# One transfer for the last context rows of four batches, and q moved by batch over 128 partitions

## The chip, the cores and the metric

The kernel runs on one core of a Trainium2 chip. The metric is the device time of that core in microseconds. Of the kernel before there are three runs: 1287.83, 1288.2 and 1289.85 us, with a median of 1288.2 us.

## What is computed

The input `x` has 128 batches of 32 rows by 1024 columns, all in float32. Three layers follow one another, each with a residual, and each reads the layer norm of the running sum:

```python
x = x + xattn(layernorm(x), ctx_1024, ctx_1024, 0, mask)
x = x + s4(layernorm(x), Lambda, p, q, Vc, Ct, Bp, D, log_step)
x = x + ffn(layernorm(x), A_w, B_w, Wq_w, keys)

# xattn: 32 heads of 32 columns, 8 groups of keys and values, 257 context rows of 256 columns a batch
scores = einsum('bsgrd,btgd->bgrst', xq, xk) / sqrt(32) + mask
out = einsum('bgrst,btgd->bsgrd', softmax(scores), xv)
# s4: a causal convolution over the last axis with one kernel of 1024 numbers, made from the parameters
# ffn: 64 experts of rank 8, gated by a top-16 router, between two dense products
```

The change touches the first layer alone: the last (257th) context row of each batch, and the way the normalised rows `xq` come into the layout that the scores need.

## The kernel before

A tile is 128 rows: four batches of 32. There are 32 tiles. The program is written out by hand for each engine, in an `iteration(it, odd)` that each engine runs for `it` from 2 to 30, with hand-ordered calls before and behind it. An iteration works on several tiles at once: scores and exponentials of tile `it`, the output and the convolution of tile `it - 1`, the experts of tile `it - 2`, and loads and layer norm of tiles `it + 1` and `it + 2`. Engines wait for each other only by semaphores, each in the order in which its calls stand.

- **SyncE issues every transfer**, one after the other, each once its semaphores allow. In an iteration this is the order around the change: `load_last(it + 1)` (L404), `store_q(it + 1)` (L391), `load_keys(it + 1, 0)` (L365), `move_q(it + 1)` (L397), `load_keys(it + 1, 1)`, `load_context(it, 3)` (L358), `load_keys(it + 1, 2)`, `load_x(it + 2)` (L384), `load_context(it, 1)`.
- **The last context row** of a batch is not in the score matmuls, which take 256 rows. `load_last` brings it into `vl`, repeated over the batch's 32 partitions. GpSimd multiplies it with `xq` in `last_product` (L1087, the product itself is L1093) and uses it again in `last_share` (L1136). `vl` has two halves, used in turn, and `load_last(tile)` waits for the last use of the half two tiles before, among others `tm_done` of `residual`, on GpSimd.
- **q**: ScalarE normalises `xq` in place (`q_norm`, L854). `store_q` writes it to the DRAM tensor `turn_q` (batch, row, column). `move_q` waits for that and reads it back into `qx`, where partition 32 c + s holds quarter c of row s, for the four batches one after the other: 4 KB a partition in pieces of 1 KB. VectorE's `q_turn(tile, h)` (L1391, the transpose is L1394) waits for all of `q_moved`, ScalarE's `q_high` and GpSimd's `q_low` (L1084) split the result in two parts `qs`, and TensorE's `scores(it, b)` (L574) multiplies them with the keys `kt`.
- **VectorE's other work** near `q_turn`: `maximum(it, n)` (L1387), which takes a 256-wide maximum of the scores for ScalarE's `exp` (L840), and `q_stats(tile, k)` (L1417), which waits for the load of `xq` of a later tile. In an iteration `q_turn(it + 1, 0)` stands between `maximum(it, 24)` and `maximum(it, 25)`, and `q_stats(it + 2, 0)` between `maximum(it, 27)` and `maximum(it, 28)`.

A transfer raises its semaphore by 16 when it is through, so the waits count 64 for four transfers.

Of the kernel before, what the change touches and what calls it, by code (L numbers as in the profile page):

```python
# [22 lines left out]
BATCHES, SEQ, DIM = 128, 32, 1024  # L23
CTX_LEN, CTX_DIM = 257, 256
# [3 lines left out]
P = 128  # L28
BPT = P // SEQ
TILES = BATCHES // BPT  # L30
HALVES = 2
GPH = GROUPS // HALVES
# [68 lines left out]
def at(tile, per, k):  # L101

    return tile * per + k
# [8 lines left out]
def build(nc, io):  # L112
    ctx = ExitStack()
    with ctx:
        def sb(name, shape, dt=F32):
            return ctx.enter_context(nc.sbuf_tensor(name, shape, dt))

        def sem(name):
            return ctx.enter_context(nc.semaphore(name))
# [12 lines left out]
        qx = sb("qx", [P, BPT, HALVES, REP, HEAD_DIM])  # L132
# [19 lines left out]
        vl = sb("vl", [P, 2, CTX_DIM])  # L152
# [27 lines left out]
        turn_q = nc.dram_tensor("turn_q", [BPT, SEQ, DIM], F32, kind="Internal").ap()  # L180
# [7 lines left out]
        q_moved = sem("q_moved")  # L188
# [6 lines left out]
        vl_loaded = sem("vl_loaded")  # L195
# [74 lines left out]
        context = io["ctx_1024"]  # L270
# [44 lines left out]
        def _(sp):  # L315
# [81 lines left out]
            def move_q(tile):  # L397
                sp.wait_ge(q_stored, at(tile, 16, 16))
                if at(tile, 2, 0) > 0:
                    sp.wait_ge(qr_done, at(tile, 2, 0))  # L400
                for quad in range(GPH):
                    sp.dma_start(qx[SEQ * quad:SEQ * (quad + 1), :, :, :, :].rearrange("p b h r d -> p b (h r d)"),
                                 turn_q.rearrange("b s (q c) -> s b q c", q=GPH)[:, :, quad, :]).then_inc(q_moved, 16)

            def load_last(tile):
                if at(tile, 4, -5) > 0:
                    sp.wait_ge(tm_done, at(tile, 4, -5))
                if at(tile, 2, -1) > 0:
                    sp.wait_ge(lp_done, at(tile, 2, -1))
                for c in range(BPT):  # L410
                    sp.dma_start(vl[SEQ * c:SEQ * (c + 1), tile % 2, :],
                                 context[tile * BPT + c:tile * BPT + c + 1, 2 * P, :]
                                 .broadcast_to([SEQ, CTX_DIM])).then_inc(vl_loaded, 16)

            def store_last(tile):
                sp.wait_ge(lm_done, at(tile, 2, 2))
# [25 lines left out]
            def iteration(it, odd):  # L442
                turn_last(it)
                if on(it - 3):
                    store(it - 3)
                if on(it - 1):
                    move_den(it - 1, 2)
                    load_context(it - 1, 2)
                    load_residual(it - 1)
                load_context(it, 0)  # L450
                if on(it - 1):
                    move_den(it - 1, 3)
                if on(it + 1):
                    load_last(it + 1)
                    store_q(it + 1)
                    load_keys(it + 1, 0)
                    move_q(it + 1)
                    load_keys(it + 1, 1)
                load_context(it, 3)
                if on(it + 1):  # L460
                    load_keys(it + 1, 2)
                if on(it + 2):
                    load_x(it + 2)
                load_context(it, 1)
                move_den(it, 1)
                if on(it + 1):
                    store_last(it + 1)
                move_den(it, 0)
                if on(it + 1):
                    load_keys(it + 1, 3)  # L470
            load_x(0); load_router(); load_mask(); load_s4(); load_wide(); load_weight(0); load_weight(1)
            load_last(0); load_context(0, 2); clear_kernel(); load_keys(0, 0); load_context(0, 0); load_weight(2)
            store_q(0); load_keys(0, 1); load_last(1); move_q(0); load_x(1); load_weight(3); load_keys(0, 2)
            store_last(0); load_keys(0, 3); turn_last(0); store_q(1); load_weight(4); load_keys(1, 0); load_weight(5)
            move_q(1); load_keys(1, 1); store_last(1); move_den(0, 0); load_keys(1, 2); load_context(0, 3)
            load_context(0, 1); load_x(2); load_context(1, 0); move_den(0, 1); load_weight(6); load_keys(1, 3)
            load_weight(7); turn_last(1); move_den(0, 2); load_keys(2, 0); load_residual(0); move_den(0, 3)
# [567 lines left out]
        def _(pool):  # L1045
# [40 lines left out]

            def last_product(tile, h):  # L1087
                if h == 0:
                    pool.wait_ge(vl_loaded, at(tile, 64, 64))
                pool.wait_ge(xq_used, at(tile, 2, 2))  # L1090
                pool.wait_ge(lm_done, at(tile, 2, h))
                v = vl[:, tile % 2, :].rearrange("p (q h d) -> p h q d", q=GPH, h=HALVES)[:, h, :, :].unsqueeze(1).broadcast_to([P, REP, GPH, HEAD_DIM])
                pool.tensor_tensor(lastp[:, :, :, :], xq[:].rearrange("p (q h r d) -> p h r q d", q=GPH, h=HALVES, r=REP)[:, h, :, :, :], v, ALU.mult).then_inc(lp_done, 1)  # L1093
# [53 lines left out]
            def iteration(it, odd):  # L1147
# [19 lines left out]
                if on(it + 1):  # L1167
                    last_product(it + 1, 0)
                    last_sum(it + 1, 0)
                    last_mask(it + 1, 0)  # L1170
# [3 lines left out]
                if on(it + 1):  # L1174
                    last_product(it + 1, 1)
                k_low(it, 3)
                if on(it + 1):
                    last_sum(it + 1, 1)
                    last_mask(it + 1, 1)
                    q_low(it + 1, 0)  # L1180
                    k_low(it + 1, 0)
            row_scale(0, 0); last_product(0, 0); last_sum(0, 0); last_mask(0, 0); last_product(0, 1); last_sum(0, 1)
            last_mask(0, 1); k_low(0, 0); k_low(0, 1); q_low(0, 0); row_scale(0, 1); q_low(0, 1); k_low(0, 2)
            last_product(1, 0); last_sum(1, 0); last_mask(1, 0); last_shift(0, 0); last_product(1, 1); last_sum(1, 1)
# [511 lines left out]
```

## Time and profile before

| | us |
|---|---|
| median of three runs | 1288.2 |
| runs | 1287.83 to 1289.85 |
| the profiled execution's own time | 1290.52 |
| its span | 1288.6 |
| TensorE busy | 1232.9 (96%) |
| VectorE busy | 959.7 (74%) |
| ScalarE busy | 1122.9 (87%) |
| GpSimd busy | 825.4 (64%) |
| transfers, mean share of 16 DMA engines (main queue) | 40.9% |

The span runs from the first to the last instruction of the program; the profiled execution took 1.9 us more than its span and 2.3 us more than the median of the runs. Busy time is what an engine spent in instructions; register, semaphore and DMA-issuing instructions don't count. A share is an average over stages with different limits, so the stages have to be read one by one.

### The profile page before, as it was taken

What the parts mean: (1) busy time and instruction counts of PE and PEld (TensorE: products, weight loads), DVE (VectorE), ACT (ScalarE), POOL (GpSimd) and SP (SyncE); (2) the same over time, 40 slices, a digit from 0 to 9 for tenths busy, and PEclk for the clock granted to TensorE, in tenths of its full rate; (3) what the DMA queues carried; (4) which work ended last, traced back from release to release, by engine and by line L of the source; (5) the groups of instructions that cost most, each with busy time, mean ns of one, the idle gap of its engine ahead of it and who ended that gap; (6) DMA issues with size and microseconds to landing.
All of it is one profiled execution on the core that took longest, in us unless ns stands there. A gap on an engine that the chain in (4) does not pass through costs nothing.

```text
span 1288.6 us, 41515 instructions
## 1 busy us (share of the span) xinstructions
PE 1232.9 (96%) x13676; PEld 1083.1 (84%) x13676; DVE 959.7 (74%) x3424; ACT 1122.9 (87%) x3337; POOL 825.4 (64%) x1259
## 2 busy tenths in 40 slices
PE   3679999999999999999999999999999999999997
PEld 2558888888888888888888888888888888888886
DVE  6977777777777777877777777677777877877753
ACT  5889999998999999999999999989999999999841
POOL 4447676776667677666767766676777666777520
PEclk9979999999999999999999999999999999999999
DMA  7443443443344444434544433453443344444210
GB/s 237 134 127 93 151 155 122 130 133 125 119 148 152 124 130 132 129 123 141 155 122 131 147 124 118 134 154 123 131 151 123 122 128 154 132 125 132 61 60 33
DMA packets 150103, 166.38 MB, mean 129 GB/s; under 512 B 58217, under 2 KB 116082, under 8 KB 149890
## 3 DMA queue, kind: packets, MB, share of 16 engines
q1 hardware_dynamic: 149890, 163.72, 40.9%
q8 instruction: 112, 1.84, 0.6%
q14 instruction: 101, 0.83, 0.2%
HBM read 128.50 MB, written 34.08 MB: 126 GB/s over the span
## 4 chain that ended last, share of the span: by engine, by line
PE 76%; DVE 5%; DMA 4%; POOL 4%; ACT 4%; issue 3%; SPq 2%; DVEq 0%; ACTq 0%; POOLq 0%
PE ps_p L562 22%; PE ps_p L633 15%; PE ps_p L661 12%; PE ps_p L648 12%; PE ps_p L594 8%; PE ps_s L574 7%; ACT pr L840 2%; DMA dn<-den 2%; DMA xq<-in_x 1%; POOL lastp L1093 1%; DVE ms L1387 1%; SPq L381 1%; ACT pts L772 1%; DMA vl<-in_ctx 1%; POOL lastp L1103 1%
## 5 line engine op out<-in xcount | busy, mean ns | idle before, releaser
L840 ACT ACTIVATE pr<-ms,negmax 128x256 f32<-128x256 f32 x1024 | 512.6, 504 | 17.3 <-DVE negmax L1387 17.3
L1387 DVE CUSTOM_DVE_ANT_0 ms<-ps_s,neg_mask,last 128x256 f32<-128x256 f32 x1024 | 447.0, 473 | 7.1 <-PE ps_s L574 6.2
L772 ACT ACTIVATE pts<-ps_p 128x512 f32<-128x512 f32 x512 | 298.3, 590 | 45.8 <-PE ps_p L562 29.1
L562 PE MATMUL ps_p<-ident,pr 128*128 128x128 f32 x2048 | 296.5, 280 | 10.4 <-ACT pr L840 5.1
L562 PEld LDWEIGHTS ps_p<-ident,pr 128*128 128x128 f32 x2048 | 229.1, 142 | 48.0 <-issue 17.4
L840 ACT ACTIVATION_READ_ACCUMULATOR pr<-ms,negmax 128x1 f32 x1024 | 199.6, 195 | 0.0
L1061 POOL TENSOR_TENSOR kt<-kr,kt 128x512 fp32r<-128x512 f32 x128 | 164.9, 1288 | 24.1 <-ACT kt L772 24.1
L648 PE MATMUL ps_p<-wa_hi,ut_hi 128*128 128x288 f32 x512 | 159.6, 312 | 1.4 <-DVE ut_lo L1203 1.4
L648 PE MATMUL ps_p<-wa_lo,ut_hi 128*128 128x288 f32 x512 | 151.8, 296 | 0.0
L648 PE MATMUL ps_p<-wa_hi,ut_lo 128*128 128x288 f32 x512 | 151.7, 296 | 0.0
L1203 DVE TENSOR_TENSOR ut_lo<-ps_p,ut_hi 128x512 fp32r<-128x512 f32 x128 | 87.7, 690 | 74.8 <-ACT ut_hi L772 74.5
L1103 POOL TENSOR_TENSOR lastp<-lastp 128x256 f32<-128x256 f32 (+4 forms) x320 | 128.1, 400 | 22.7
L594 PE MATMUL ps_p<-pts,cx 128*32 128x128 f32 x4096 | 139.8, 277 | 2.8 <-DVE wb_lo L1215 2.3
L633 PE MATMUL ps_p<-strip_hi,ut_hi 128*128 128x512 f32 (+2 forms) x384 | 135.5, 353 | 0.0
L574 PE MATMUL ps_s<-kt,qs 32*128 32x256 f32 x3072 | 128.1, 297 | 5.3 <-DVE negmax L1387 3.0
L633 PE MATMUL ps_p<-strip_hi,ut_lo 128*128 128x512 f32 (+2 forms) x384 | 133.1, 347 | 0.0
L633 PE MATMUL ps_p<-strip_lo,ut_hi 128*128 128x512 f32 (+2 forms) x384 | 132.9, 346 | 0.0
L1084 POOL TENSOR_TENSOR qs<-qr,qs 128x512 fp32r<-128x512 f32 x64 | 82.6, 1290 | 69.6 <-ACT qs L772 69.6
L574 PEld LDWEIGHTS ps_s<-kt,qs 32*128 32x128 f32 x3072 | 101.9, 187 | 28.6 <-issue 24.9
L594 PEld LDWEIGHTS ps_p<-pts,cx 128*32 128x32 f32 x4096 | 105.0, 110 | 24.8 <-issue 21.5
L1136 POOL TENSOR_TENSOR tmp<-vl,dn 128x512 f32<-128x512 f32 x64 | 69.1, 1079 | 80.6 <-DVE dn L1447 80.6
L772 ACT ACTIVATE ut_hi<-ps_p 128x512 fp32r<-128x512 f32 x128 | 75.3, 592 | 51.0 <-PE ps_p L562 50.9
(139 smaller groups left out, 2584.6 us busy)
## 6 DMA issues: line engine op xcount, KB each, us to landing
cx<-in_ctx SPq DMA_DIRECT2D x128, 256.0 KB, 3.9
kr<-in_keys SPq DMA_DIRECT2D x128, 256.0 KB, 3.0
xq<-in_x SPq DMA_DIRECT2D x32, 512.0 KB, 4.3
turn_q<-xq SPq DMA_DIRECT2D x32, 512.0 KB, 2.9
qx<-turn_q SPq DMA_DIRECT2D x128, 128.0 KB, 2.9
xr<-in_x SPq DMA_DIRECT2D x32, 512.0 KB, 3.9
out_x<-tmp SPq DMA_DIRECT2D x32, 512.0 KB, 3.2
dn<-den SPq DMA_DIRECT2D x512, 2.0 KB, 2.3
```

The source lines that it names most:

```text
L562: mm = pe.transpose(into[:, j * P:(j + 1) * P], source, ident[:, :])
L574: mm = pe.matmul(ps_s[:, quad, h * SW:(h + 1) * SW], qs[rs, it % 2, q_part, b, h, :, :].rearrange("p r s -> p (r s)"), kt[rs, b, k_part, h ...
L594: mm = pe.matmul(product("o", b, it)[HEAD_DIM * q:HEAD_DIM * (q + 1), h * P:(h + 1) * P], cx[:, b, j, g * HEAD_DIM:(g + 1) * HEAD_DIM], pt ...
L633: mm = pe.matmul(product("y", k, tile)[:, o0:512], u[:, c, :], s[:, s0:s0 + w], start=(c == 0 and j == 0), stop=(c == 4 * k + 3 and j == 2 ...
L648: mm = pe.matmul(product("f", k, tile)[:, 0:ZB], u[:, c, :], w[:, c, k * ZB:(k + 1) * ZB], start=(c == 0 and j == 0), stop=(c == FC - 1 an ...
L661: mm = pe.matmul(product("b", k, tile)[:, :], u[:, c, :], w[:, c, k * 512:(k + 1) * 512], start=(c == 0 and j == 0), stop=(c == BC - 1 and ...
L772: return act.activation(out, in_, ACT.Copy, scale=scale)
L840: act.activation(pr[:, b % 2, g, :], ms[:, n % MS, :], ACT.Exp, bias=negmax[:, n % MS:n % MS + 1], scale=-1.0, accum_out=den[:, b, g:g + 1 ...
L1061: pool.tensor_tensor(kt[:, b, 1, :, :], kr[:, at(tile, BPT, b) % KRS, :, :], kt[:, b, 0, :, :].bitcast(F32), ALU.subtract).then_inc(kl_don ...
L1103: pool.tensor_tensor(near, near, far, ALU.add).then_inc(ls_done, 1)
L1203: return dve.tensor_tensor(lo, source, hi.bitcast(F32), ALU.subtract).then_inc(done, 1)
L1387: dve.tensor_tensor_reduce(ms[:, n % MS, :], ps_s[:, g % GPH, g // GPH * SW:(g // GPH + 1) * SW], neg_mask[:, 0:SW], 1.0, last[:, it % 2, ...
```

## The change

`move_q` has four transfers as before, but each now brings one batch to all 128 partitions, where each brought one quarter of the columns of all batches to 32 partitions. The pieces are the same 512 of 1 KB a tile. The source of a transfer is now written with the quarter `q` outermost (4 entries), then the row `s` (32), then 256 columns; it was the row outermost (32), then the batch (4), then 256 columns.

`load_last` now has one transfer a tile where it had four. The source is 4 batches outermost, each repeated 32 times with a step of zero, then 256 columns; the destination is 128 partitions. It was 32 repeats of one row to 32 partitions. GpSimd's wait counts 16 a tile now, not 64.

```diff
-                for quad in range(GPH):
-                    sp.dma_start(qx[SEQ * quad:SEQ * (quad + 1), :, :, :, :].rearrange("p b h r d -> p b (h r d)"),
-                                 turn_q.rearrange("b s (q c) -> s b q c", q=GPH)[:, :, quad, :]).then_inc(q_moved, 16)
+                for b in range(BPT):
+                    sp.dma_start(qx[:, b, :, :, :].rearrange("p h r d -> p (h r d)"),
+                                 turn_q[b, :, :].rearrange("s (q c) -> q s c", q=GPH)).then_inc(q_moved, 16)
...
-                for c in range(BPT):
-                    sp.dma_start(vl[SEQ * c:SEQ * (c + 1), tile % 2, :],
-                                 context[tile * BPT + c:tile * BPT + c + 1, 2 * P, :]
-                                 .broadcast_to([SEQ, CTX_DIM])).then_inc(vl_loaded, 16)
+                sp.dma_start(vl[:, tile % 2, :],
+                             context[tile * BPT:(tile + 1) * BPT, 2 * P, :].unsqueeze(1)
+                             .broadcast_to([BPT, SEQ, CTX_DIM])).then_inc(vl_loaded, 16)
...
-                    pool.wait_ge(vl_loaded, at(tile, 64, 64))
+                    pool.wait_ge(vl_loaded, at(tile, 16, 16))
```

On SyncE, in an iteration, these are the transfers around the two places before; the sizes are those of the destination, partitions first.

```order
L381 DMA dn<-den 32x16 x4
L411 DMA vl<-in_ctx 32x256 x4
L395 DMA turn_q<-xq 128x1024
L369 DMA kr<-in_keys 128x512
L402 DMA qx<-turn_q 32x4x256 x4
L369 DMA kr<-in_keys 128x512
L362 DMA cx<-in_ctx 128x2x256
L369 DMA kr<-in_keys 128x512
L389 DMA xq<-in_x 128x1024
```

And this is the same place with the change:

```order
L381 DMA dn<-den 32x16 x4
L410 DMA vl<-in_ctx 128x1x256
L395 DMA turn_q<-xq 128x1024
L369 DMA kr<-in_keys 128x512
L402 DMA qx<-turn_q 128x1x256 x4
L369 DMA kr<-in_keys 128x512
L362 DMA cx<-in_ctx 128x2x256
L369 DMA kr<-in_keys 128x512
L389 DMA xq<-in_x 128x1024
```

Nothing stands in another place: three issues a tile are gone, and the order of the rest is the same. The other engines' instructions are unchanged.

## Rows read from the trace of the kernel before

**Rows 1.** The page, section 1: busy us, share of the span, instructions.
```profile
PE 1232.9 (96%) x13676; PEld 1083.1 (84%) x13676; DVE 959.7 (74%) x3424; ACT 1122.9 (87%) x3337; POOL 825.4 (64%) x1259
```
**Rows 2.** Busy time by stretch; the header gives the columns.
```profile
core 0: us, PE busy (x) PEld busy (x) DVE busy (x) ACT busy (x) POOL busy (x), PEclk, DMA share, GB/s
...
103.00:1196.00 1093.00, 1089.30 (x12305) 961.95 (x12304) 833.33 (x3038) 1002.84 (x3015) 749.72 (x1139) 1.00 0.43 133
```
**Rows 3.** Waits in total; SyncE's own first: us, times, longest.
```profile
SPq L411 <- POOL tmp L1136: 189.0, 30, 7.3
...
POOL lastp L1093 <- DMA vl<-in_ctx: 9.4, 6, 7.6
...
PEld ps_s L574 <- POOL kt L1061: 3.7, 15, 0.6
```
**Rows 4.** Transfers issued: count, KB each, median us from issue to landing.
```profile
vl<-in_ctx SPq DMA_DIRECT2D x128, 32.0 KB, 1.8
```
**Rows 5.** Packets in 169.1:171.2, 651.05:652.85, 98.3:100.3; q1: packets, MB, share of 16 engines.
```profile
DMA packets 489, 0.45 MB, mean 216 GB/s; under 512 B 47, under 2 KB 489, under 8 KB 489
q1 hardware_dynamic: 489, 0.45, 72.3%
...
DMA packets 184, 0.14 MB, mean 79 GB/s; under 512 B 60, under 2 KB 183, under 8 KB 183
q1 hardware_dynamic: 183, 0.13, 23.0%
...
q1 hardware_dynamic: 100, 0.00, 2.7%
```
**Rows 6.** SyncE's timeline, tile 4 and tile 17: start us, us, transfer.
```profile
168.27 1.83 SPq L402 DMA_DIRECT2D qx<-turn_q  x4
...
656.22 1.76 SPq L402 DMA_DIRECT2D qx<-turn_q  x4
...
663.60 0.38 SPq L389 DMA_DIRECT2D xq<-in_x  x1
```
**Rows 7.** VectorE's timeline, the first use of q and of x: tiles 4, 17.
```profile
176.51 0.71 DVE L1394 STREAM_TRANSPOSE qr<-qx 128x512 f32<-128x512 f32 x1
...
179.52 0.69 DVE L1417 BATCH_NORM_STATS2 lns<-xq 128x6 f32<-128x512 f32 x1
...
664.87 0.71 DVE L1394 STREAM_TRANSPOSE qr<-qx 128x512 f32<-128x512 f32 x1
...
667.88 0.68 DVE L1417 BATCH_NORM_STATS2 lns<-xq 128x6 f32<-128x512 f32 x1
```
**Rows 8.** GpSimd's and TensorE's timelines behind them: end of q's split, next scores.
```profile
672.22 1.28 POOL L1084 TENSOR_TENSOR qs<-qr,qs 128x512 fp32r<-128x512 f32 x1 [0.57 <-ACT qs L772]
...
674.64 0.98 PE L574 MATMUL ps_s<-kt,qs 32*128 32x256 f32 x24
```
**Rows 9.** VectorE's and TensorE's timelines where x came late.
```profile
293.25 0.69 DVE L1417 BATCH_NORM_STATS2 lns<-xq 128x6 f32<-128x512 f32 x1 [1.45 <-DMA xq<-in_x]
...
298.08 0.63 PE L562 MATMUL ps_p<-ident,x 128*128 128x128 f32 x4 [0.32 <-DVE x L1462]
```
**Rows 10.** The first 20 us: busy time by stretch, then SyncE's timeline, then the chain.
```profile
10.00:18.00 8.00, 2.28 (x11) 2.31 (x12) 5.65 (x12) 5.29 (x8) 2.11 (x2) 1.00 1.04 371
18.00:20.00 2.00, 2.00 (x11) 1.88 (x11) 1.08 (x1) 0.60 (x1) 1.76 (x4) 1.00 0.59 204
...
5.78 3.15 SPq L411 DMA_DIRECT2D vl<-in_ctx  x4
...
11.72 8.77 DMA kr<-in_keys
```
**Rows 11.** Tile 1's q: SyncE's and VectorE's timelines, and busy time by stretch.
```profile
47.22 2.51 SPq L402 DMA_DIRECT2D qx<-turn_q  x4
...
54.55 0.71 DVE L1394 STREAM_TRANSPOSE qr<-qx 128x512 f32<-128x512 f32 x1
...
50.00:55.00 5.00, 3.35 (x54) 2.54 (x57) 4.86 (x22) 5.00 (x20) 1.64 (x3) 1.00 0.68 151
```

## The prediction

> **What bounds the kernel now.** I read the page first: TensorE is busy for 96% of the span, ScalarE for 87%, VectorE for 74% [rows 1]. Then the stretches: from 103 to 1196 us TensorE is busy for 1089.3 of 1093.0 us [rows 2]. So over 29 tiles of some 37.5 us only 3.7 us are lost; a time saved on another engine or queue is worth nothing there, and a delay costs only what is over its slack. Elsewhere (the first 100 us, before the pipeline is full) the transfers and VectorE count. Next SyncE's waits: it stood 189.0 us before `load_last`, waiting for GpSimd [rows 3]. A queue that waits so much is not short of issue time. Last the timelines around q, to see by how much each transfer is early.
>
> **What is removed: three issues a tile.** An issue takes some 0.43 us on SyncE (four in 1.76 us [rows 6]), so 3 x 0.43 = 1.3 us a tile. After `load_last` SyncE mostly waits for the next thing anyway, so I count zero. The one who may gain is GpSimd: it waited for `vl` 6 times, 9.4 us together, of which the start is 7.6 us [rows 3], and TensorE's weight loads waited for GpSimd's `kt` 3.7 us in 15 times. The rest, 1.8 us of GpSimd's waits, is the ceiling in the steady part; behind GpSimd there is slack again, so I take 0.3 us of TensorE's time.
>
> **What is changed: how the packets spread over the DMA engines.** The bytes and packets are the same. A q transfer now goes at a DMA share of 72.3%, counted over 16 engines, with other traffic small [rows 5], so its pieces lie on all of them. What the new patterns do is not in this trace: none of its transfers has a source with 4 entries outermost. The two bounds are 16 engines as now, and four engines, one for each outermost entry. Under the first nothing changes. I take the second, since the outermost entry is the natural unit to divide by (the old ones had 32 rows there), and since it is the bound that can hurt.
>
> The Trainium skill, "DMA: Bandwidth & Descriptors", section "Why a DMA increments its semaphore by 16 and not by 1", says that the number of engines is the largest number up to 16 that divides the slowest non-unit dimension of both patterns, which would be 4 here, the lowest four; its section "Rules for kernel authors" warns of just such a leading zero-stride broadcast. It speaks against this change; by it the four-engine bound holds, and no row of this trace shows it.
>
> **The price of a packet.** Small packets cost 2.7% x 16 x 2.0 us / 100 = 8.6 ns [rows 5]. A 1 KB packet of q costs (72.3% x 16 x 2.1 us - 47 x 0.0086) / 442 = 54 ns, one of `vl` (23.0% x 16 x 1.8 - 60 x 0.0086) / 123 = 50 ns. I take 52 ns. Bigger ones go by the full stretch: 371 GB/s over 16 engines [rows 10] is 23 GB/s each, 0.73 us for the 16 KB that an engine carries of a `kr` load, 1.47 us for its 32 KB of `xq`. What a transfer costs beside its packets is 1.8 us less two packets = 1.7 us, by `vl` [rows 4].
>
> **q, on four engines.** 512 packets on 4 engines are 128 each, 128 x 52 = 6.7 us, where it was 32 each. Last landing: 1.7 + 6.7 = 8.4 us behind the first issue. It is needed after 176.51 - 168.27 = 8.24 us in tile 4, after 664.87 - 656.22 = 8.65 us in tile 17 [rows 6, 7]. So VectorE waits for 0 to 0.2 us: the change eats the whole slack and stops there.
>
> **x, behind q on the same four engines.** `load_x` is issued 7.38 us after q [rows 6], and then these engines have still `kr`, `cx` (16 x 52 ns = 0.83 us) and `kr` to do: 8.4 + 0.73 + 0.83 + 0.73 + 1.47 = 12.1 us behind q's issue. It is needed after 11.25 us (tile 4) to 11.66 us (tile 17) [rows 6, 7]. VectorE, in order, then waits for 0.5 to 0.9 us, and its next maxima, ScalarE's exponentials and the second half of q come later by as much. What is late next is `scores(it + 1, 0)`: GpSimd has q's split ready at 672.22 + 1.28 = 673.50 us, TensorE begins at 674.64, a slack of 1.1 us [rows 8]. A case of it is in the trace: a wait of 1.45 us for x cost TensorE 0.3 us [rows 9], which is the same slack. So 0.5 to 0.9 us are covered, and the steady part costs **nothing**; if the cover were gone, each tile would pay all of it, some 20 us. With 50 ns the wait is 0.2 to 0.6 us, with 54 ns 0.8 to 1.2 us, the edge.
>
> **vl, on four engines.** 32 packets each, 1.7 us, against four issues over 1.3 us now: it lands at about the same time. Hidden, as now, by GpSimd's work of the tile before.
>
> **The start.** From 10 to 18 us all engines are full (share 1.04), then 0.59 [rows 10]. Four of them get 24 packets more from `vl` of tile 0: 24 x 52 ns = 1.25 us. The `kr` load that the chain runs through for 8.77 us [rows 10] is queued behind. Its bounds: 1.25 us later, or up to 2.0 us earlier, since SyncE's four issues took 3.15 us there and one takes at most 1.15. As the engines are full, an earlier issue only lengthens the queue: I take +1.25 us. Tile 1's q is issued at 47.22 and needed at 54.55, after 7.33 us [rows 11], so VectorE waits 1.1 us; but ScalarE is the full one there (5.00 of 5.00 us), fed by maxima already made. Bounds 0 to 1.1, I take 0, by that row.
>
> **Sum.** 1.25 - 0.3 + 0 = +1.0 us. The profiled execution took 1290.5 us and would take 1291.5; it stands 2.3 us over the median, so for the median 1288.2 + 1.0 = **1289.2 us**. Own range of this case 1287.0 to 1291.5 (below: no loss at the start and the 0.3 us; above: 1.25 and 1.1 us at the start, and an edge of 1 us over the slack in some tiles). What a measurement can tell from no change is 0.2%, 2.6 us.
>
> **The rivals.**
> - **The slack is overrun (slower).** Everything as above, but packets on four full engines cost more, or SyncE is held up behind their queues. It decides from a DMA wait of 1.1 us on VectorE a tile. For it: 54 ns already reaches 1.2 us. Against it: the engines then carry one stream, with little contention. At the wait of [rows 9] in each of 28 tiles: 28 x 0.3 = 9 us, 1288.2 + 1.25 + 9 = 1298.5 us. At 58 ns x would land at 8.4 + 0.8 + 3.8 = 13.0 us, a wait of 1.7, a loss of 0.6 us: 17 us, 1306 us. Chance 0.33.
> - **The pieces go to 16 engines as before (the change does only what saves issues).** For it: no row speaks against it. Then there is -0.3 us and nothing at the start: 1287.9 us. Chance 0.12.
> - **The start was short of issue time (faster).** The queue has a gap that the 2.0 us of SyncE's time fills, and `kr` lands up to 2.0 us earlier; with GpSimd's 1.8 us passed on in full: 1288.2 - 3.8 = 1284.4 us. The share of 1.04 speaks against it. Chance 0.08.
>
> **How the numbers follow.** The forecast has 0.47, of which 0.04 lies over +2.6 us. Slower is 0.33 + 0.04 = 0.37, faster 0.08, the same 0.43 + 0.12 = 0.55. The range leaves out the faster rival and the far end of the slower one, some 0.2 together: 1286.5 to 1300.
>
> **What would show it.** Right: q lands 8 to 8.8 us behind its first issue, the DMA share stays at a quarter in that stretch and not 72%; VectorE's wait for x goes from 10.5 us in all to 15 to 25 us, some small waits for q appear; TensorE stays busy for over 1088 us of 1093 in the same stretch; the first scores come 1 us later. Wrong: q's landing unchanged (16 engines); x's wait over 1.1 us in most tiles and TensorE waiting behind `qs`, `z` or the maxima; or an issue on SyncE that takes microseconds, because a queue is full.

## The result and the profile after

The changed kernel takes **1301.7 us** in the median of four runs (1296.34 to 1301.99), the kernel before 1288.0 (1285.33 to 1289.85): a ratio of **1.0098, 95% interval 1.0066 to 1.013**. Timed again later it was 1.0120 (1.0094 to 1.0145). So it is slower by some 14 to 16 us, and the forecast of 1289.2 us is wrong; 1301.7 lies outside its range of 1286.5 to 1300.0. The profiled execution took 1301.71 us, with a span of 1299.9, against 1290.52 and 1288.6 before: 11.3 us longer.

The page of the changed kernel, section 1, answers to [rows 1]; under it the busy time of the stretch of [rows 2]:

```profile
PE 1237.5 (95%) x13676; PEld 1083.0 (83%) x13676; DVE 959.0 (74%) x3424; ACT 1126.0 (87%) x3337; POOL 825.7 (64%) x1259
```
```profile
103.00:1196.00 1093.00, 1081.88 (x12208) 951.36 (x12207) 826.11 (x3006) 994.40 (x2977) 742.31 (x1124) 1.00 0.42 131
```

TensorE is idle for 11.1 us of the stretch, where it was for 3.7, and gets through 97 matmuls fewer (12208 against 12305, 0.8%). The loss is in the steady part. TensorE's timelines of before (the first two rows) and of the changed kernel (the last two) show where the scores of tile 3 and of tile 31 begin:

```profile
148.93 0.98 PE L574 MATMUL ps_s<-kt,qs 32*128 32x256 f32 x24
...
1199.11 0.98 PE L574 MATMUL ps_s<-kt,qs 32*128 32x256 f32 x24
```
```profile
147.77 0.98 PE L573 MATMUL ps_s<-kt,qs 32*128 32x256 f32 x24
...
1210.68 0.98 PE L573 MATMUL ps_s<-kt,qs 32*128 32x256 f32 x24
```

These 28 tiles took 1050.18 us and take 1062.91: +12.7 us, or 0.45 us a tile. What lies before them and behind them did not lose: 1288.6 - 1050.2 = 238.4 us before, 1299.9 - 1062.9 = 237.0 now.

Over just these 28 tiles, the same work in both, TensorE's idle time goes from 3.7 us (1050.18 less 1046.49 busy) to 11.1 (1062.91 less 1051.80), 7.4 us more. The rest is busy time, and it lies in the matmuls of one line, L633 before and L632 now, which multiply `strip` with the two halves of `ut` for the convolution. Their rows, first before, then after (us; busy us of matmuls and of weight loads; granted clock, DMA share, GB/s):

```profile
148.93:1199.11 1050.18, 191.94 (x1008) 166.24 (x1008) 1.00 0.43 133
```
```profile
147.77:1210.68 1062.91, 197.77 (x1008) 167.46 (x1008) 1.00 0.42 131
```

They are busy for 5.8 us more. Together that is 13.2 us, all of the 12.7. The tile read below shows why both belong to one place.

The chain of waits, by engine, first before and then after:

```profile
PE 76%; DVE 5%; DMA 4%; POOL 4%; ACT 4%; issue 3%; SPq 2%; DVEq 0%; ACTq 0%; POOLq 0%
```
```profile
PE 54%; DMA 16%; ACT 9%; DVE 6%; issue 5%; POOL 5%; SPq 5%; DVEq 0%; ACTq 0%; POOLq 0%
PE ps_p L561 16%; PE ps_p L632 11%; PE ps_p L647 9%; DMA qx<-turn_q 7%; PE ps_p L593 7%; PE ps_p L660 6%; ACT pr L839 5%; PE ps_s L573 5%; DMA turn_q<-xq 3%; DMA xq<-in_x 3%; DMA dn<-den 2%; SPq L402 2%; SPq L381 2%; ACT xq L853 2%; ACT pts L771 1%
```

TensorE held three quarters of the chain and holds half. The transfers of q (`qx<-turn_q`) have 7% of it; before they were not among its lines. The waits in total (engine, line, what it waited for: us, times, longest) answer to [rows 3]; lines behind `load_last` are one lower than before:

```profile
DVE qr L1393 <- DMA qx<-turn_q: 20.9, 24, 2.5
DVE lns L1416 <- DMA xq<-in_x: 10.1, 14, 4.6
PE ps_p L632 <- DVE ut_lo L1202: 9.5, 15, 1.5
POOL lastp L1092 <- DMA vl<-in_ctx: 8.6, 1, 8.6
```

The first line is new. VectorE waits for q in most tiles, 20.9 us in all. The third is new too: TensorE waits for `ut_lo`, a product of VectorE that has nothing to do with q. VectorE's wait for x is no longer than before over the whole run (10.5 us there); in the stretch of [rows 2] it is 5.6 us in 13 times, against 4.7 in 8. What the forecast took for the next thing late, TensorE's scores waiting for q's split, is in no row. GpSimd waits for `vl` only once, at the start.

**One tile read through.** Tile 8's q in the changed kernel, from the timelines of SyncE, VectorE and TensorE (start us, us, engine, line, operation; in brackets the idle time before it and what ended it):

```profile
320.24 2.26 SPq L402 DMA_DIRECT2D qx<-turn_q  x4
...
328.82 0.28 PE L632 MATMUL ps_p<-strip_hi,ut_lo 128*128 128x256 f32 x1
...
328.84 0.71 DVE L1393 STREAM_TRANSPOSE qr<-qx 128x512 f32<-128x512 f32 x1 [1.84 <-DMA qx<-turn_q]
...
329.85 0.69 DVE L1202 TENSOR_TENSOR ut_lo<-ps_p,ut_hi 128x512 fp32r<-128x512 f32 x1
...
330.59 0.49 PE L632 MATMUL ps_p<-strip_hi,ut_hi 128*128 128x512 f32 x1 [1.49 <-DVE ut_lo L1202]
```

q lands 328.84 - 320.24 = 8.6 us behind its first issue. VectorE has been standing in front of its transpose for 1.84 us. Behind the transpose in its queue come `maximum(it, 25)` and then `u_low(it - 1, 1)`, which makes the second half of `ut_lo` for the convolution of the tile before. That ends at 330.54, and TensorE, through with the first half at 329.10, starts the second at 330.59. Before, in tile 17, the same pieces stood like this:

```profile
665.88 0.68 DVE L1203 TENSOR_TENSOR ut_lo<-ps_p,ut_hi 128x512 fp32r<-128x512 f32 x1
...
666.85 0.28 PE L633 MATMUL ps_p<-strip_hi,ut_lo 128*128 128x256 f32 x1
666.97 0.39 PE L633 MATMUL ps_p<-strip_hi,ut_hi 128*128 128x512 f32 x1
```

`ut_lo` was ready at 666.56 and was used at 666.97: **0.4 us of slack** (0.34 to 0.42 us in tiles 3 to 29 of this trace). I had not looked at this place.

The last matmul of the first half and the first of the second half stand 0.12 us apart here (666.85 and 666.97) and 1.77 us apart in the tile above (328.82 and 330.59). So the wait costs 1.65 us where the idle time says 1.49, since the matmul in front of it is recorded as busy for its whole 0.28 us; and the one behind it takes 0.49 us in place of 0.39. That is how a wait for `ut_lo` puts time into the busy column too.

**How late q is.** Before, q was through 4.4 us (median) after its first issue, by the semaphore events of the trace in tiles 3 to 30, with 3.7 us to spare in the median tile. Now it is 8.8 us (8.3 to 9.6), and VectorE gets to its transpose after 8.35 us, as before (8.25). SyncE's issues of four q transfers take 2.26 us where they took 1.76 [rows 6]. Median landings of the transfers queued behind q, section 6 of the page, first before, then after:

```profile
cx<-in_ctx SPq DMA_DIRECT2D x128, 256.0 KB, 3.9
kr<-in_keys SPq DMA_DIRECT2D x128, 256.0 KB, 3.0
xq<-in_x SPq DMA_DIRECT2D x32, 512.0 KB, 4.3
```
```profile
cx<-in_ctx SPq DMA_DIRECT2D x128, 256.0 KB, 4.8
kr<-in_keys SPq DMA_DIRECT2D x128, 256.0 KB, 4.3
xq<-in_x SPq DMA_DIRECT2D x32, 512.0 KB, 5.5
```

**How many engines.** In the middle of a q transfer of the changed kernel, 660.9 to 662.9 us, the packets of the main queue take 22.5% of 16 engines' time, where it was 72.3% [rows 5]:

```profile
q1 hardware_dynamic: 144, 0.14, 22.5%
```

The packet counts say it more exactly. The page of before, then of the changed kernel:

```profile
DMA packets 150103, 166.38 MB, mean 129 GB/s; under 512 B 58217, under 2 KB 116082, under 8 KB 149890
```
```profile
DMA packets 146646, 166.36 MB, mean 128 GB/s; under 512 B 54761, under 2 KB 112626, under 8 KB 146434
```

The small packets are 3456 fewer. If each transfer ends with one small packet for each engine that it uses, then q on four engines saves 4 transfers x 12 engines x 32 tiles = 1536, and `vl` saves (4 x 16 - 4) x 32 = 1920: together 3456. The Trainium skill, "DMA: Bandwidth & Descriptors", section "Why a DMA increments its semaphore by 16 and not by 1", says that only the engines that a transfer uses post an increment, and that their number is the largest up to 16 that divides both patterns' slowest dimension; by that rule it is four, and the count agrees to the packet.

### The profile page after: what moved, and what is told of

Read it like the earlier page. It is cut to its first block, busy times and chain, and to the rows that moved or that the text cites. A ratio compares the mean times of both kernels' runs of the same rounds, so it can differ in the third digit from the quotient of the medians.

```text
span 1299.9 us, 41419 instructions
## 1 busy us (share of the span) xinstructions
PE 1237.5 (95%) x13676; PEld 1083.0 (83%) x13676; DVE 959.0 (74%) x3424; ACT 1126.0 (87%) x3337; POOL 825.7 (64%) x1259
## 3 DMA queue, kind: packets, MB, share of 16 engines
q8 instruction: 112, 1.84, 0.6%
## 4 chain that ended last, share of the span: by engine, by line
PE 54%; DMA 16%; ACT 9%; DVE 6%; issue 5%; POOL 5%; SPq 5%; DVEq 0%; ACTq 0%; POOLq 0%
PE ps_p L561 16%; PE ps_p L632 11%; PE ps_p L647 9%; DMA qx<-turn_q 7%; PE ps_p L593 7%; PE ps_p L660 6%; ACT pr L839 5%; PE ps_s L573 5%; DMA turn_q<-xq 3%; DMA xq<-in_x 3%; DMA dn<-den 2%; SPq L402 2%; SPq L381 2%; ACT xq L853 2%; ACT pts L771 1%
## 5 line engine op out<-in xcount | busy, mean ns | idle before, releaser
L632 PE MATMUL ps_p<-strip_hi,ut_hi 128*128 128x512 f32 (+2 forms) x384 | 137.9, 359 | 9.9 <-DVE ut_lo L1202 9.5
L632 PE MATMUL ps_p<-strip_hi,ut_lo 128*128 128x512 f32 (+2 forms) x384 | 133.1, 347 | 0.0
L632 PE MATMUL ps_p<-strip_lo,ut_hi 128*128 128x512 f32 (+2 forms) x384 | 132.7, 346 | 0.0
L1470 DVE TENSOR_TENSOR tmp<-ps_p,x 128x512 f32<-128x512 f32 x64 | 44.2, 691 | 98.9 <-PE ps_p L660 98.8
```

The lines of the kernel that those rows point to most:

```text
L632: mm = pe.matmul(product("y", k, tile)[:, o0:512], u[:, c, :], s[:, s0:s0 + w], start=(c == 0 and j == 0), stop=(c == 4 * k + 3 and j == 2 ...
```

## The experiments

The kernel before was timed beside each on the same chip; ratios are to it.

### Each part alone: `vl_only`, `q_only`

`vl_only` is the changed kernel with the old q:

```diff
-                for b in range(BPT):
-                    sp.dma_start(qx[:, b, :, :, :].rearrange("p h r d -> p (h r d)"),
-                                 turn_q[b, :, :].rearrange("s (q c) -> q s c", q=GPH)).then_inc(q_moved, 16)
+                for quad in range(GPH):
+                    sp.dma_start(qx[SEQ * quad:SEQ * (quad + 1), :, :, :, :].rearrange("p b h r d -> p b (h r d)"),
+                                 turn_q.rearrange("b s (q c) -> s b q c", q=GPH)[:, :, quad, :]).then_inc(q_moved, 16)
```

> Only the last context rows come by one transfer; q is moved as before. Theory A (q on four engines lands about 8.8 us behind its first issue, later than VectorE's transpose needs it at 8.2 to 8.7 us): the whole loss goes, 1287 to 1289 us, TensorE idle under 5 us between 103 and 1180 us, no wait for q on VectorE. Rival B (the four lowest engines' extra load from both changes delays the transfers behind it, x above all): a part of the loss stays, 1290 to 1293 us. The count of packets falls by 1920 (128 x 16 less 32 x 4 completion packets) if a transfer posts one on each engine it uses and these transfers use four.

Measured: 1286.15 us in the median (12 runs), ratio **0.9992** (0.9977 to 1.0006). The small packets are 58217 - 56297 = 1920 fewer. One transfer on four engines in place of four on 16 is worth nothing that can be told.

```profile
DMA packets 148182, 166.37 MB, mean 129 GB/s; under 512 B 56297, under 2 KB 114162, under 8 KB 147970
```

`q_only` is the same exchange the other way: the kernel before with the new q.

> Only q is moved by batch; the last context rows come by four transfers as before. Theory A: the whole loss stays, 1299 to 1303 us, VectorE waits about 20 us in all for q. Rival B: between before and the change, 1293 to 1298 us. The count of packets falls by 1536 (128 x 16 less 128 x 4).

Measured: 1305.92 us (5 runs), ratio **1.0157** (1.0134 to 1.0180), which is above the 1299 to 1303 us expected. The small packets are 1536 fewer (56681), and the two new waits are there:

```profile
DVE qr L1394 <- DMA qx<-turn_q: 24.9, 25, 3.1
PE ps_p L633 <- DVE ut_lo L1203: 13.3, 15, 1.9
```

So **the whole loss is q's**. q alone even seemed worse than both parts together (1.0157 against 1.0098), which `after_again` below takes up.

### By batch, but on 16 engines: `q_batch_16`

Both parts of the change stay, and a q transfer still brings one batch to 128 partitions. The DRAM tensor is now laid out as batch, quarter, row, so that a batch reads as 128 rows in one dimension; the store is four transfers of 32 partitions, in pieces of 1 KB:

```diff
-    sp.dma_start(turn_q.rearrange("b s c -> (b s) c"), xq[:, :]).then_inc(q_stored, 16)
+    for b in range(BPT):
+        sp.dma_start(turn_q[b, :, :, :].rearrange("q s c -> s q c"),
+                     xq[SEQ * b:SEQ * (b + 1), :].rearrange("s (q c) -> s q c", q=GPH)).then_inc(q_stored, 16)
...
-                                 turn_q[b, :, :].rearrange("s (q c) -> q s c", q=GPH)).then_inc(q_moved, 16)
+                                 turn_q[b, :, :, :].rearrange("q s c -> (q s) c")).then_inc(q_moved, 16)
```

The waits for the store count 64 in place of 16.

> Both changes stay, but turn_q is laid out by batch, quarter, row, so that the read of a batch to 128 partitions has one outermost dimension of 128; the store takes four transfers of 32 partitions with pieces of 1 KB. Theory A (the number of engines is the cause): q lands 4.4 to 5.5 us behind its first issue, 1286 to 1290 us, the packet count is near that of before less 1920 plus the store's own (384 more data packets and 48 more completions a tile). Rival C (it is the spread over 128 partitions or the order of the rows that is slow): q still lands after over 8 us and the loss of 12 us stays.

Measured: 1287.07 us (12 runs), ratio **1.0002** (0.9983 to 1.0022). q lands 3.9 us behind its first issue, and VectorE waits for it nowhere. To move q by batch costs nothing; the outermost dimension of its source does. The order of the pieces in DRAM changes along with it, but the kernel before reads the old order in 4.4 us on 16 engines. The layout also makes the store's pieces smaller and its issues four, and even that is hidden.

### Half the dose, and its control: `q_half`, `q_six_16`

`q_half`, from the kernel before: two batches by batch on four engines, two by quarter, in six transfers.

```diff
+                for b in range(2):
+                    sp.dma_start(qx[:, b, :, :, :].rearrange("p h r d -> p (h r d)"),
+                                 turn_q[b, :, :].rearrange("s (q c) -> q s c", q=GPH)).then_inc(q_moved, 16)
                 for quad in range(GPH):
-                    sp.dma_start(qx[SEQ * quad:SEQ * (quad + 1), :, :, :, :].rearrange("p b h r d -> p b (h r d)"),
-                                 turn_q.rearrange("b s (q c) -> s b q c", q=GPH)[:, :, quad, :]).then_inc(q_moved, 16)
+                    sp.dma_start(qx[SEQ * quad:SEQ * (quad + 1), 2:4, :, :, :].rearrange("p b h r d -> p b (h r d)"),
+                                 turn_q.rearrange("b s (q c) -> s b q c", q=GPH)[:, 2:4, quad, :]).then_inc(q_moved, 16)
```

The waits for q count 96 a tile here, and in `q_six_16` below, in place of 64.

> The last context rows as before; batches 0 and 1 of q by batch (64 KB-pieces: 64 packets on each of four engines), batches 2 and 3 by quarter over 16 engines, six transfers. Theory A: half the dose, q lands 1.7 + (64 + 16) x 0.052 = 5.9 to 6.5 us behind its first issue, before VectorE needs it at 8.2: no wait for q, time as before, 1287 to 1290 us. A rival in which each packet on the four engines costs TensorE something in proportion: half the loss, 1293 to 1296 us.

Measured: 1295.15 us (4 runs), ratio **1.006** (1.004 to 1.0081). That is a miss. q lands after 7.0 us, later than I expected, yet VectorE hardly waits for it:

```profile
DVE lns L1420 <- DMA xq<-in_x: 11.5, 12, 4.6
PE ps_p L565 <- DVE x L1456: 4.0, 9, 0.8
DVE qr L1397 <- DMA qx<-turn_q: 0.9, 2, 0.8
```

Six issues take 3.1 us of SyncE, so the loss could have been theirs. `q_six_16` has the six issues without the four engines:

```diff
-                for quad in range(GPH):
-                    sp.dma_start(qx[SEQ * quad:SEQ * (quad + 1), :, :, :, :].rearrange("p b h r d -> p b (h r d)"),
-                                 turn_q.rearrange("b s (q c) -> s b q c", q=GPH)[:, :, quad, :]).then_inc(q_moved, 16)
+                for quad, b0, b1 in ((0, 0, 4), (1, 0, 4), (2, 0, 2), (2, 2, 4), (3, 0, 2), (3, 2, 4)):
+                    sp.dma_start(qx[SEQ * quad:SEQ * (quad + 1), b0:b1, :, :, :].rearrange("p b h r d -> p b (h r d)"),
+                                 turn_q.rearrange("b s (q c) -> s b q c", q=GPH)[:, b0:b1, quad, :]).then_inc(q_moved, 16)
```

> The kernel before, but q by quarter in six transfers (two quarters whole, two in two pieces each), every transfer with 32 rows outermost, so on 16 engines: the issue time of the half dose (3.1 us) without its four-engine pieces. The half dose took 1295.2 us, 1.006 of before. Theory A (engines are the cause, of the half dose too): q lands 4.5 to 6 us behind its first issue, x at 11 to 12 us: 1286.5 to 1290 us. Rival C (SyncE's two further issues and what they push back, kr, cx and x, cost the half dose its time): x 12 us or more behind q's first issue, VectorE waits over 6 us for it, 1292 to 1297 us.

Measured: 1286.82 us (12 runs), ratio **1.0001** (0.998 to 1.0022). SyncE's timeline has about the same issue time (3.0 us against 3.1), and q lands after 4.6 us all the same:

```profile
652.47 2.99 SPq L402 DMA_DIRECT2D qx<-turn_q  x6
```

So issue time costs nothing here. By exclusion the half dose's loss is put down to its two transfers on four engines, but no trace shows how they cost 7.7 us. The half dose's profiled execution waits for q only 0.9 us. From the scores of tile 3 to those of tile 31 it takes 1052.9 us, where the two profiles of the kernel before take 1050.2 and 1052.6 (`before_again`), and its matmuls with `strip` are busy for 192.0 us, as before. So its steady part shows no loss beyond what these two profiles differ by. The loss rests on four run times (1292.09 to 1295.92, against 1283.86 to 1291.04 in 23 runs of the kernel before beside it), and its cause stays open.

### VectorE's order: `turn_later`, `turn_later_before`

If the cost is that the transpose stands in front of `u_low(it - 1, 1)`, it must shrink when the two change places. ScalarE's half goes along:

```diff
                 maximum(it, 24)
-                if on(it + 1):
-                    q_turn(it + 1, 0)
                 maximum(it, 25)
                 if on(it - 1):
                     u_low(it - 1, 1)
+                if on(it + 1):
+                    q_turn(it + 1, 0)
                 maximum(it, 26)
...
                 exp(it, 24)
+                exp(it, 25)
                 if on(it + 1):
                     q_high(it + 1, 0)
-                exp(it, 25)
                 exp(it, 26)
```

> The change, with VectorE's q_turn(it + 1, 0) put behind maximum(it, 25) and u_low(it - 1, 1), 1.0 us later, and ScalarE's q_high(it + 1, 0) behind exp(it, 25). Theory A2 (the loss comes because u_low, which TensorE's convolution needs within 0.4 us, stands behind the transpose that waits for q): TensorE's waits for ut_lo go, VectorE hardly waits for q (it lands after 8.8 us, needed then after 9.2 to 9.7), 1288 to 1293 us. Rival B2 (any lateness of q, kr, cx and x on the four engines costs, wherever the wait stands): 1298 to 1303 us, the waits come back in front of the scores or the maxima.

Measured: 1297.76 us (6 runs), ratio **1.0083** (1.005 to 1.0116), between the two expectations and nearer to the rival's. The wait for `ut_lo` is gone, and VectorE's for q with it, but for the start. What stops VectorE now is the load of x, `xq<-in_x`. TensorE's weight loads wait for the sum that VectorE writes at L1461 (named `x` too: the residual behind the convolution, not the input), which they did for 1.8 us in 5 times before:

```profile
DVE lns L1416 <- DMA xq<-in_x: 12.4, 16, 5.1
...
PEld ps_p L561 <- DVE x L1461: 6.9, 20, 0.6
...
DVE qr L1393 <- DMA qx<-turn_q: 2.2, 2, 1.9
```

The wait that I had named was real, and it covered a second one. The control, `turn_later_before`, has the same edit on the kernel before:

> Control: the same move in the kernel before, where q is in time. Both theories: 1286 to 1290 us, no difference to before over 0.2 %. If it is faster or slower by more, the move has an effect of its own that has to be taken off the run beside it.

Measured: 1288.45 us (12 runs), ratio **1.0016** (0.9992 to 1.0040). The order alone is worth nothing that can be told. In the stretch of [rows 2] VectorE's wait for x is 7.3 us in `turn_later` (the first row) and 1.2 us in this control (the second), so it is the late transfers that make it:

```profile
DVE lns L1416 <- DMA xq<-in_x: 7.3, 15, 1.1
```
```profile
DVE lns L1417 <- DMA xq<-in_x: 1.2, 3, 0.7
```

### SyncE's order: `keys_first`

The changed kernel, with the second `kr` and the last `cx` ahead of q, so that they don't lie between q and x on the four engines:

```diff
                     load_keys(it + 1, 0)
-                    move_q(it + 1)
                     load_keys(it + 1, 1)
                 load_context(it, 3)
                 if on(it + 1):
+                    move_q(it + 1)
                     load_keys(it + 1, 2)
```

> The change, with the kr and cx loads that were issued behind q issued ahead of it, while SyncE waits for the store of q. Their 1.6 us of work on each engine is then done before q's pieces. Theory A2: q lands as late as before behind its issue (8.8 us), TensorE's waits for ut_lo stay, 1298 to 1303 us, though VectorE's waits for x shrink. Rival B2 (the backlog behind q is what costs): x lands about 1.5 us earlier and most of the loss goes, 1290 to 1295 us.

Measured: 1299.46 us (6 runs), ratio **1.0086** (1.0057 to 1.0115). x is nearly in time now (1.0 us of its wait lies in the stretch of [rows 2], the rest at the start), but q is as late, and the two waits stay:

```profile
DVE qr L1393 <- DMA qx<-turn_q: 19.3, 24, 2.3
PE ps_p L632 <- DVE ut_lo L1202: 8.6, 11, 1.7
...
DVE lns L1416 <- DMA xq<-in_x: 5.7, 3, 4.8
```

The matmuls with `strip` are busy for 196.9 us in tiles 3 to 31, as in the changed kernel. The queue behind q is thus not the cost by itself, any more than VectorE's order is.

### Both orders together: `both_moved`

The edits of `turn_later` and `keys_first` in one kernel. q is still on four engines.

> The changed kernel with both edits together: VectorE's turn of q stands behind the maximum and u_low that follow it (ScalarE's q_high likewise), and SyncE issues the second kr and the last cx ahead of q. Each alone left the time at 1297.8 and 1299.5 us against the changed kernel's 1301.7. Theory A3 (the loss is made of two waits that covered for one another: q in front of ut_lo, and x): q lands some 8.5 us behind its issue, VectorE waits for q under 3 us and for x under 4 us in tiles 3 to 31, and what is left is the 0.3 us between ql and scores: 1291 to 1295 us, steady part 1052 to 1056 us. Rival B3 (q that lands 4 us later costs the same wherever VectorE turns it, since scores of the next tile are then late): 1296 to 1300 us, steady part over 1057 us.

Measured: 1288.81 us (12 runs), ratio **1.0022** (1.0005 to 1.0040). Each edit alone left 1.0083 and 1.0086 of the 1.0098; together they leave 1.0022, so some four fifths of the loss are back. That is also faster than the 1291 to 1295 us expected. q still lands 8.5 us behind its issue, and VectorE gets to it after 9.8. Waits and the stretch of [rows 2]:

```profile
DVE lns L1416 <- DMA xq<-in_x: 6.3, 5, 5.0
...
DVE qr L1393 <- DMA qx<-turn_q: 2.7, 3, 2.1
```
```profile
103.00:1196.00 1093.00, 1090.36 (x12338) 961.95 (x12337) 832.34 (x3034) 1006.25 (x3013) 750.42 (x1137) 1.00 0.41 132
```

TensorE is busy for 1090.36 us, more than before the change (1089.30). From the scores of tile 3 to those of tile 31 it takes 1049.7 us, against 1050.2 before, and the matmuls with `strip` are busy for 191.9 us again. VectorE's wait for x is 1.3 us in the stretch, and no engine waits in that stretch for `kr` or `cx`, here or in `turn_later`; so it is x that the new order of SyncE helps. This closes the account of the steady part: the late q costs what waits behind it in VectorE's order, the late x costs next, and once both places have slack again, four engines cost almost nothing. Some 0.2% are left in the run times, just clear of zero, and are not placed.

### Repeats, and a candidate: `before_again`, `after_again`, `vl_keys_first`

`before_again` is the kernel before, profiled once more for the start.

> The kernel before once more, for a second profile: whether the start (scores of tile 2 begin at 111.7 us in the first one, with TensorE at half clock for 10.2 and 3.4 us) is the same each time. If the 3 to 4 us by which the kernels with the one vl transfer reach tile 2 earlier come from that transfer, it begins again at 111 to 113 us; if they come from the clock by chance, it may be 108.

Measured: 1287.03 us, one run. The scores of tile 2 begin at 107.6 us, against 111.7 in the first profile and 109.3 in the changed kernel. The granted clock stood at half for 6.8 us in one stretch behind 65 us here, and for 10.2 + 3.4 us in the first profile: the start varies by 4 us in the same kernel. The steady part, from the scores of tile 3 to those of tile 31, varies too: 1052.6 us here, 1050.2 in the first profile.

`after_again` is the changed kernel, timed again:

> The changed kernel unchanged, timed again in five rounds on this chip. q alone measured 1.0157 of before, both parts 1.0098 from four runs, vl alone 0.9992. Theory A (vl is worth nothing beside q too, and the two figures differ by chance of few runs): ratio 1.011 to 1.016, so that its interval meets that of q alone. Rival E (the three issues that vl no longer takes are worth some 0.5% once q is late): ratio 1.006 to 1.011, an interval that ends below 1.013 again. Under both, VectorE waits for q in over 20 of the tiles and q lands 8.5 to 9 us behind its first issue.

Measured: 1302.52 us (6 runs), ratio **1.0120** (1.0094 to 1.0145). Its interval overlaps that of q alone (1.0134 to 1.0180), so a gain of `vl` beside q is not shown. VectorE waits for q 19 times, where over 20 were expected.

`vl_keys_first` has the change of `vl`, the old q and SyncE's new order. It was to beat both kernels.

> vl by one transfer, q as in the kernel before, and SyncE issues the second kr and the last cx ahead of q, so that x finds an emptier queue. The candidate for a kernel that beats both. Theory A (before lost only 3.7 us of TensorE in the steady part, of which x has a share): x lands under 10 us behind q's issue, VectorE waits under 1 us for it, q's slack of 4 us pays for 0.9 us of later issue: 1284.5 to 1287.5 us, faster by 0 to 0.2%. Rival D (the waits of TensorE in before have nothing to do with x, and a kr or cx ahead of q pushes something else back): 1287.5 to 1290 us.

Measured: 1286.68 us (12 runs), ratio **1.0005** (0.9985 to 1.0026). Its profile has TensorE busy for 1091.50 us of the stretch, 2.2 more than before, but the times don't show it. No version beat the kernel before.

## Why the prediction was wrong

**Engines: right.** Four engines for either part, taken against the bound of 16. The share in the stretch and the packet counts show it.

**q's landing: about right, a little short.** The forecast was 8.4 us; the median is 8.8 (8.3 to 9.6). The formula started from the first issue and added one fixed time and 128 packets of 52 ns. It had no room for SyncE's four issues, which take 0.5 us longer than before; that would cover the 0.4 us, but no run takes it apart. VectorE's wait was to be 0 to 0.2 us a tile. It is 0.4 us in the difference of the medians, and in the steady stretch it adds up to 16.7 us over 29 tiles, 0.6 us each.

**The step that failed: "the change eats the whole slack and stops there", and the slack of 1.1 us in front of `scores(it + 1, 0)`.** I followed q to the work that needs q and priced the delay by the slack there. VectorE executes in order, so a wait for q also holds all that stands behind the transpose, and the next thing that TensorE needs from it is `ut_lo`, one `maximum` further on, with 0.4 us of slack. The order was in the code and the times in the timelines of the trace of before. `both_moved` against `keys_first` shows it: the only difference is that order (and ScalarE's, whose half of q's split moved along), and the ratio goes from 1.0086 to 1.0022. What the runs show in place of "nothing" in the steady part is 12.7 us, 0.45 us a tile, all of it at that place.

**x: its size was off, its place also.** x was to land 12.1 us behind q's issue, and does (12.1 in the median), but VectorE's wait for it hardly grew (4.7 to 5.6 us in the stretch of [rows 2]), since VectorE already comes later by its wait for q. Once that wait is away (`turn_later`), x's is 7.3 us in the stretch, 0.5 us each in 15 times, and TensorE loses by it: the cover of 1.1 us was not there either. The case that was to confirm it, [rows 9], is of another place: there TensorE waits for VectorE's sum `x` (L1462), not in front of the scores. That 1.45 - 0.3 us comes near the 1.1 us says nothing of the scores.

**The removed issues and `vl`: right.** Ratio 0.9992 alone. SyncE still stands 189.9 us in front of `load_last` (189.0 in [rows 3]).

**Two small slips in the sum.** 16 KB at 23 GB/s are 0.71 us and 32 KB are 1.41, where 0.73 and 1.47 are written; and the terms as written add up to 12.2 us for x, not 12.1. Neither moves the forecast.

**The start, +1.25 us: cannot be told.** In the chain the `kr` transfer of the first 20 us takes 9.69 us where it took 8.77 [rows 10], which has the forecast's sign and most of its size; the first scores of the steady part come 1.2 us earlier all the same. As the start varies by 4 us in the same kernel, neither says what the change does there.

```profile
11.56 9.69 DMA kr<-in_keys
```

**The rivals.** "The slack is overrun" is what came, with a chance of 0.33 and a time of 1298.5 to 1306 us. Its price was near by luck of place: 0.3 us a tile from a wait for x in [rows 9], against 0.45 measured, through another wait. Its threshold, a DMA wait of 1.1 us a tile, was wrong: some 0.4 us are enough. The forecast gave most weight to a case whose slack was read at one consumer only. The forecast's own sign of error, TensorE waiting behind "`qs`, `z` or the maxima", named the wrong places as well.

## What to carry to other kernels

When a transfer becomes later, find the engine that waits for it, and read down that engine's order: the delay is priced by the least slack among everything queued behind the wait, not by the slack of the transfer's own consumer. One cure at a time may show little where two waits cover for each other; test them together before ruling either out. And look at the outermost dimension of both patterns of every transfer: the same bytes in the same pieces took 8.8 us with 4 entries outermost and 3.9 with 128.

## What was not expected of the hardware

**A short wait can cost TensorE twice.** In the profile of `after_again` TensorE's granted clock fell twice in the steady part, each time behind a wait for `ut_lo`. The stretches (us; busy us of PE, PEld, DVE, ACT, POOL; granted clock, DMA share, GB/s):

```profile
401.80:405.20 3.40, 1.39 (x10) 1.18 (x8) 1.43 (x4) 1.25 (x5) 0.01 (x1) 1.00 0.97 315
405.20:408.60 3.40, 3.08 (x7) 2.48 (x8) 3.31 (x12) 2.57 (x10) 2.29 (x2) 0.51 0.22 59
```

And TensorE's timeline there:

```profile
405.52 0.80 PE L632 MATMUL ps_p<-strip_hi,ut_hi 128*128 128x512 f32 x1 [2.33 <-DVE ut_lo L1202]
406.11 0.63 PE L632 MATMUL ps_p<-strip_lo,ut_hi 128*128 128x512 f32 x1
...
408.67 0.39 PE L632 MATMUL ps_p<-strip_lo,ut_hi 128*128 128x512 f32 x1
```

Behind a wait of 2.33 us the same matmul takes 0.63 us instead of 0.39, at a granted clock of 0.51 (1.2 GHz in place of 2.4). The other fall there stood behind a wait of 1.83 us, one in `q_only` behind 1.92; behind the 1.49 us of the tile read above the clock stayed at 1.00. The length of the wait alone does not decide it: `q_only` has one of 1.84 us behind which the clock stayed at 1.00 too.

```profile
257.47 0.50 PE L633 MATMUL ps_p<-strip_hi,ut_hi 128*128 128x512 f32 x1 [1.84 <-DVE ut_lo L1203]
```

No other profile has such a fall between 103 and 1196 us. From the scores of tile 3 to those of tile 31 it is 1066.5 us in `after_again` and 1062.9 in the first profile, 3.6 us more. Of these 1.7 us are idle time (12.8 against 11.1) and 1.9 us busy time, so at most half is the clock's. How often it happens in unprofiled runs is not known.

**The number of engines can be read from the count of packets.** With one small packet at the end of each transfer for each engine used, the count of packets under 512 B comes out exactly in every variant: 1920 fewer for `vl` and 1536 fewer for q on four engines, 256 more for the half dose, 1024 more for six transfers on 16 engines.
